# Reordering a hand-laid engine schedule in a gated-delta-rule and expert kernel

## The chip, the core and the metric

The kernel runs on one core of a Trainium2 chip. The metric is the device time of one execution in microseconds; lower is better. The core has five instruction queues that matter here: TensorE (PE, with its weight loads shown as PEld), VectorE (DVE), ScalarE (ACT), GpSimd (POOL) and SyncE (SP), which issues the DMAs. Each queue runs its instructions strictly in the order in which they were written; semaphores tie the queues together.

## What is computed

The reference is one transformer layer on 4 sequences of 256 tokens with 256 features: a gated delta rule attention with 16 key heads and 32 value heads of width 128, then a mixture of 34 small experts. Cut to what matters here:

```python
qkvz = x @ W_qkvz.T                      # 16 heads, 6*128 columns each
qkv  = silu(conv1d_causal(qkv, conv_w))  # 4 taps per channel
q, k = rmsnorm(q), rmsnorm(k)
M = strictly_lower(k_beta @ k.T * decay)
T = inverse(I + M)                       # solve_triangular in the reference
v_new = T @ v_beta - (T @ k_beta_exp_g) @ state
out   = q_exp_g @ state + (q @ k.T * decay) @ v_new
state = state * exp(g_last) + k_decayed.T @ v_new
y = (rmsnorm(out) * norm_w * silu(z)) @ W_out.T
x = x + layernorm(y)
x = x + layernorm(experts(layernorm(x)))
```

## The kernel before

The attention stage is cut into 64 **units**. A unit is one pair (group, batch): a group is one key head with its two value heads, and there are 16 groups of 4 batches, so a group has unit 0 to unit 3. The state is carried in two chunks of 128 tokens per unit.

Two streams of work run side by side in the attention stage.

The **unit stream** does the delta rule of one unit. Its backbone is a triangular inverse built up in seven levels, here called the ladder. For level n:

- TensorE forms `x n` (function `x`, L619) into `X_BANK`, from `n16` and the part `t16` of the inverse;
- ScalarE copies it to `x16`, called `xe n` (L954; the last one, `xe 6`, is L956);
- TensorE forms `w n` (L639 for one product, L647 for its transpose), from `x16` and `u16`;
- VectorE merges them with predicated copies, called `t n` (L1199) and `u n` (L1212, for `u 6` a plain copy, L1215).

`w 0` (L630, L632) opens the ladder of a unit. It overwrites the banks of the unit ahead and therefore waits for that unit's `u 6`. So ladders of two units never overlap. Between its rungs stand the other steps of the units just behind: the solve against the state (`y0` L663, `y1` L675 to L681, `y2` L687 on TensorE, `g` L966, `vn` L972 and `v0s` L979 on ScalarE, `rr` L1225 and `r1h` L1232 on VectorE), the carried product `p` (L696), the output `o` (L711, L714), the mean of squares (`sqr` L986 on ScalarE, `hsum` L1395 on GpSimd, `ss` L725 on TensorE, `ln` and `rex` L993 and L999 on ScalarE), the gating (`hz` L1241, `ht` L1250), the output projection `proj` (L734) and its accumulation `acc` (L1257). For the next unit there are the key products `kk` (L607, L610), `mask` (L1175), `cap`, `exp` and `cross` (L915, L929, L936 on ScalarE), the decayed matrix `nt` (L1184), its f16 copies `n16` (L943) and, on GpSimd, `nl` (L1413), the factors `at` (L1421) and `qx` (L1428), and `eye`, which resets `t16` and `u16` (L1403, L1407).

The **front stream** prepares the next group. It has 18 fills of two PSUM banks: `fill n` and `rest n` are the two halves of a projection of 512 tokens (L559, three products each), `evict n` is ScalarE's copy out of the bank (L858 or L864), and three `tap`s per fill on VectorE (L1139) are the convolution. Then come `silu` (L893, L898), squares on GpSimd, the norm (`nexp` L905, `nmul` L1167), transposes of v (`fill 14` to `fill 17`), the per-group scalars `sc` (L1160), and the split of the following group's weights into high and low f16 parts: `hi` on ScalarE (L886) and `lo` on VectorE (L1149). SiLU and the exponentials lie in different activation tables, and a group changes table four times (L893, L800, L864, L800).

What orders all this is not a scheduler but two tables of numbers. `SLOT` lists the steps of the unit stream once; an entry is a step, its index, and a lag in units (how many units behind the current one it belongs to). `FRONT` hangs the front stream's steps on places (unit within the group, position in `SLOT`), with the number of groups ahead. `sequence()` walks both and yields one global list. Each engine's program takes the steps that it owns out of that list, in order:

```python
def attention(engine_steps):
    for what, k, U in sequence():
        if what in engine_steps:
            engine_steps[what](U, k)
```

So a table entry matters only through the order that it gives among steps of the same engine. The waits stand inside the steps and are the same wherever a step stands.

Of the kernel before, what the change touches and what calls it, by code (L numbers as in the profile page):

```python
# [61 lines left out]

FRONT = {
    (0, 0): [("tap", 1, 1)],
    (0, 2): [("fill", 1, 1)],
# [2 lines left out]
    (0, 16): [("evict", 1, 1)],
    (0, 18): [("tap", 3, 1)],
    (0, 21): [("fill", 2, 1)],  # L70
    (0, 28): [("rest", 2, 1)],
    (0, 33): [("tap", 4, 1)],
    (0, 38): [("tap", 5, 1)],
# [5 lines left out]
    (0, 68): [("tap", 7, 1)],
    (0, 71): [("tap", 8, 1)],  # L80
    (0, 74): [("tap", 9, 1)],
    (1, 1): [("evict", 3, 1)],
    (1, 2): [("fill", 4, 1)],
    (1, 4): [("rest", 4, 1)],
    (1, 13): [("tap", 10, 1), ("evict", 4, 1)],
    (1, 16): [("fill", 5, 1)],
    (1, 18): [("tap", 11, 1)],
    (1, 27): [("evict", 5, 1)],
    (1, 28): [("rest", 5, 1)],
    (1, 30): [("tap", 12, 1)],  # L90
    (1, 38): [("tap", 13, 1)],
    (1, 46): [("tap", 14, 1)],
# [1 line left out]
    (1, 53): [("fill", 6, 1)],
    (1, 60): [("tap", 16, 1)],
    (1, 61): [("wo", 0, 1)],
    (1, 67): [("tap", 17, 1), ("rest", 6, 1), ("sq", 0, 1)],
    (1, 72): [("fill", 7, 1), ("tap", 18, 1)],
    (1, 74): [("evict", 6, 1)],
    (2, 4): [("tap", 19, 1)],  # L100
    (2, 5): [("rest", 7, 1)],
    (2, 10): [("fill", 8, 1), ("rest", 8, 1)],
    (2, 13): [("tap", 20, 1), ("evict", 7, 1)],
# [3 lines left out]
    (2, 21): [("tap", 23, 1), ("qsq", 0, 1), ("silu", 1, 1)],
    (2, 27): [("rest", 9, 1)],
    (2, 29): [("fill", 10, 1), ("silu", 2, 1)],
    (2, 31): [("rest", 10, 1), ("evict", 9, 1)],  # L110
    (2, 45): [("fill", 11, 1)],
# [1396 lines left out]
```

## Time and profile before

| | |
|---|---|
| median of 3 runs | 1440.54 us (1439.3 to 1442.4) |
| the profiled execution, its own time | 1435.98 us |
| its span, first to last instruction | 1433.7 us |
| PE busy | 1290.2 us (90%) |
| PE weight loads busy | 892.1 us (62%) |
| DVE busy | 1078.2 us (75%) |
| ACT busy | 961.3 us (67%) |
| POOL busy | 633.8 us (44%) |
| mean granted TensorE clock | 0.979 |

The attention stage fills the span up to about 1107 us and the experts run from there to the end. Busy shares over the span mix these two. Matmul ends are modelled and weight loads overlap matmuls, so the pitch between starts of neighbouring instructions, and idle time with its releaser, say more of TensorE than its busy share does.

### The profile page before, as it was taken

The numbers are of one execution on the slowest core, as the hardware profiler recorded it, in microseconds if no ns is written. First come the engines' busy times: TensorE is split into PE (matmuls) and PEld (weight loads), VectorE is DVE, ScalarE is ACT, GpSimd is POOL, SyncE is SP. The second block draws the span as 40 slices with busy tenths as digits, with TensorE's granted clock in tenths as the row PEclk, the third lists the DMA queues.
The fourth block names the chain that finished last, engine by engine and source line by source line (L and its number), as shares of the span: only waits on it lengthen the run. The fifth ranks groups of instructions, "written<-read, shape, count | busy, mean of one in ns | idle before, by whom it ended". The sixth has DMA issues, their size and how long they took to land.

```text
span 1433.7 us, 33842 instructions
## 1 busy us (share of the span) xinstructions
PE 1290.2 (90%) x11516; PEld 892.1 (62%) x11516; DVE 1078.2 (75%) x2142; ACT 961.3 (67%) x2122; POOL 633.8 (44%) x726
## 2 busy tenths in 40 slices
...
DMA packets 44656, 76.34 MB, mean 53 GB/s; under 512 B 7172, under 2 KB 26022, under 8 KB 44488
## 3 DMA queue, kind: packets, MB, share of 16 engines
...
q14 instruction: 73, 0.60, 0.1%
...
## 4 chain that ended last, share of the span: by engine, by line
PE 65%; DVE 17%; issue 8%; ACT 8%; DVEq 1%; DMA 0%; SPq 0%; POOL 0%; ACTq 0%; POOLq 0%
PE bank L559 11%; PE bank L781 8%; PE products L734 6%; DVE sil L1139 6%; PE bank L514 5%; PE products L514 4%; PE products L711 4%; PE bank L639 4%; PE products L725 3%; PE products L607 3%; PE bank L619 3%; PE bank L647 3%; DVE u L1212 2%; DVE t L1199 2%; PE bank L696 2%
## 5 line engine op out<-in xcount | busy, mean ns | idle before, releaser
L559 PE MATMUL bank<-xT,whl 128*128 128x512 f16 x1152 | 305.9, 380 | 12.8 <-DVE sil L1139 12.7
L1139 DVE SCALAR_TENSOR_TENSOR sil<-bank,cw,sil 128x510 f32<-128x510 f32 (+2 forms) x384 | 283.7, 739 | 9.9 <-ACT sil L858 5.3
L1403 POOL COPY t<-eye 128x512 f16<-128x512 f16 x64 | 39.2, 612 | 446.9 <-PE bank L647 446.9
L1199 DVE CAST_PREDICATED t<-levm,bank 128x256 f16<-128x256 uint8 x384 | 166.0, 432 | 87.2 <-PE bank L632 52.9
L954 ACT ACTIVATE x<-bank 128x256 f16<-128x256 f32 x320 | 125.5, 392 | 93.2 <-PE bank L619 89.5
L1029 ACT ACTIVATE kq<-vtok 128x512 f16<-128x512 f32 x94 | 59.2, 630 | 192.0 <-DVE vtok L1326 192.0
L1212 DVE CAST_PREDICATED u<-levm,bank 128x256 f16<-128x256 uint8 x384 | 163.6, 426 | 0.3
L619 PEld LDWEIGHTS bank<-t,n 128*128 128x128 f16 x1536 | 78.0, 97 | 103.7 <-DVE t L1199 78.3
L559 PEld LDWEIGHTS bank<-xT,whl 128*128 128x128 f16 x1152 | 92.4, 98 | 78.0 <-DVE sil L1139 16.7
L781 PE MATMUL bank<-wmhl,kq 128*128 128x256 f16 x1128 | 138.3, 273 | 0.3 <-DVE kq L1332 0.2
L619 PE MATMUL bank<-t,n 128*128 128x64 f16 x1536 | 110.0, 194 | 25.4 <-DVE t L1199 23.9
L781 PEld LDWEIGHTS bank<-wmhl,kq 128*128 128x128 f16 x1128 | 110.2, 98 | 33.2 <-DVE kq L1332 1.1
L734 PE MATMUL products<-wo,hT 128*128 128x256 f32 x512 | 128.0, 393 | 2.2 <-DVE hT L1250 2.2
L639 PEld LDWEIGHTS bank<-x,u 128*128 128x128 f16 x1280 | 62.6, 97 | 96.1 <-ACT x L954 87.4
L647 PE MATMUL bank<-u,x 128*128 128x64 f16 (+1 forms) x1536 | 109.9, 194 | 6.0 <-ACT x L956 5.1
L639 PE MATMUL bank<-x,u 128*128 128x64 f16 x1280 | 90.9, 193 | 24.3 <-ACT x L954 9.4
L734 PEld LDWEIGHTS products<-wo,hT 128*128 128x128 f32 x512 | 93.4, 193 | 13.2 <-DVE hT L1250 2.9
L858 ACT ACTIVATE sil<-bank,cw 128x512 f32<-128x512 f32 x128 | 88.5, 692 | 17.5 <-PE bank L559 15.8
L1395 POOL TENSOR_TENSOR hsq<-hsq,qsq 128x512 f32<-128x512 f32 x64 | 81.4, 1272 | 39.2 <-ACT hsq L986 39.1
L1421 POOL TENSOR_TENSOR at<-kqm,ex 128x256 f32<-128x256 f32 x128 | 93.8, 733 | 7.8 <-ACT ex L929 7.8
L1440 POOL TENSOR_SCALAR wms<-wms 128x512 f32<-128x512 f32 x47 | 31.7, 675 | 143.4 <-DMA wms<-wm 143.4
L1428 POOL TENSOR_TENSOR qx<-cross,exb 128x256 f32<-128x256 f32 x128 | 93.6, 731 | 2.9 <-ACT exb L923 2.9
...
## 6 DMA issues: line engine op xcount, KB each, us to landing
...
```

Of the source, the lines that this page charges most:

```text
L514: mm = nc.tensor.matmul(dst, stationary(h, k), moving(l, k), start=(n == 0), stop=(n == len(terms) - 1))
L559: mm = nc.tensor.matmul(dst[:, :], whl[:, h, k, col:col + HD], xT[:, l, k, half * 512:(half + 1) * 512], start=(k == 0 and m == 0), stop=( ...
L619: mm = nc.tensor.matmul(X_BANK[:, m * 64:(m + 1) * 64], N[:, m], r, start=True, stop=True)
L639: mm = nc.tensor.matmul(X_BANK[:, m * 64:(m + 1) * 64], Ut[:, m], halves(X, n)[:, m, :, 0], start=True, stop=True)
L647: mm = nc.tensor.matmul(o, l, r, start=True, stop=True)
L734: mm = nc.tensor.matmul(KB_BANK[:, c * D:(c + 1) * D], hT[:, pair(U), v, c], wo[:, q, v], start=(v == 0), stop=(v == 1))
L781: mm = nc.tensor.matmul(bank[4 + t // 2][:, (t % 2) * D:(t % 2 + 1) * D], hid[:, n % HR, h, m * P:(m + 1) * P], wmhl[:, k % HLR, l, D:2 * ...
L954: ins = nc.scalar.mul(halves(X, n)[:, :, :, 0], packed(X_BANK, n), -1.0)
L1139: nc.vector.scalar_tensor_tensor(out=dst[:, :, late:S], in0=src[:, :, 0:S - late], scalar=cw[:, q, i, 3 - late:4 - late], in1=dst[:, :, la ...
L1199: nc.vector.copy_predicated(halves(t16[:, pair(U)], n)[:, :, :, 0], by4(2 * n, n), packed(X_BANK, n)).then_inc(s_tup, 1)
L1212: nc.vector.copy_predicated(halves(Ut, n)[:, :, :, 1], by4(2 * n + 1, n), packed(WT_BANK, n)).then_inc(s_uup, 1)
L1421: nc.gpsimd.tensor_tensor(at[:, third(U), v], kqm[:, w, :, 1], ex[:, w, v], ALU.mult).then_inc(s_at, 1)
```

## The change

Only the two tables change: the order of `SLOT` and the places in `FRONT`, with some lags that stay equivalent for the data flow. No step is added or removed, no wait is changed, no buffer is resized. The table is three lines longer, so every later line number is higher by 3 in the changed kernel (L1199 becomes L1202). A few entries of the diff, to show their form and the steps spoken of below:

```diff
--- before.py
+++ after.py
@@ -49,90 +49,93 @@
...
-SLOT = [("n16", 0, 0), ("sqr", 0, 2), ("g", 0, 1), ("x", 1, 0), ("u", 0, 0), ("nl", 0, 0), ("xe", 1, 0), ("w", 1, 0),
-        ("ss", 0, 2), ("x", 2, 0), ("y1", 0, 1), ("exb", 0, 0), ("w", 2, 0), ("eye", 1, -1), ("t", 1, 0), ("u", 1, 0),
-        ("xe", 2, 0), ("ln", 0, 2), ("rex", 0, 2), ("xe", 3, 0), ("v0s", 0, 1), ("rr", 0, 1), ("t", 2, 0),
-        ("x", 3, 0), ("hz", 0, 2), ("u", 2, 0), ("y2", 0, 1), ("ht", 0, 2), ("t", 3, 0), ("w", 3, 0), ("eye", 0, -2),
-        ("at", 1, 0), ("p", 0, 1), ("x", 4, 0), ("u", 3, 0), ("qx", 1, 0), ("hsum", 0, 1), ("proj", 0, 2),
-        ("at", 0, -1), ("vn", 0, 1), ("r1h", 0, 1), ("cap", 0, -1), ("xe", 4, 0), ("row", 0, 4), ("y0", 1, 1),
-        ("w", 4, 0), ("acc", 0, 2), ("t", 4, 0), ("kk", 0, -1), ("u", 4, 0), ("x", 5, 0), ("g", 1, 1),
-        ("mask", 0, -1), ("cap", 1, -1), ("rr", 1, 1), ("qx", 0, -1), ("t", 5, 0), ("xe", 5, 0), ("y1", 1, 1),
-        ("w", 5, 0), ("exp", 0, -1), ("cross", 0, -1), ("xe", 6, 0), ("u", 5, 0), ("nt", 0, -1), ("x", 6, 0),
-        ("y2", 1, 1), ("w", 6, 0), ("o", 0, 1), ("w", 0, -1), ("u", 6, 0), ("vn", 1, 1), ("y0", 0, 0), ("t", 0, -1)]
+SLOT = [("vn", 1, 2), ("w", 6, 1), ("n16", 0, 0), ("at", 0, 0), ("sqr", 0, 2), ("o", 0, 2), ("w", 0, 0),
+        ("exb", 0, 0), ("xe", 1, 0), ("y0", 0, 1), ("t", 1, 0), ("g", 0, 1), ("u", 1, 0), ("x", 1, 0), ("w", 1, 0),
+        ("ss", 0, 2), ("x", 2, 0), ("xe", 2, 0), ("rr", 0, 1), ("ln", 0, 2), ("y1", 0, 1), ("t", 2, 0), ("hz", 0, 2),
+        ("at", 1, 0), ("row", 0, 1), ("w", 2, 0), ("rex", 0, 2), ("hsum", 0, 1), ("eye", 1, -2), ("xe", 3, 0),
+        ("u", 2, 0), ("y2", 0, 1), ("ht", 0, 2), ("v0s", 0, 1), ("x", 3, 0), ("t", 3, 0), ("w", 3, 0), ("vn", 0, 1),
+        ("u", 3, 0), ("p", 0, 1), ("x", 4, 0), ("proj", 0, 2), ("qx", 0, 0), ("xe", 4, 0), ("r1h", 0, 1),
+        ("y0", 1, 1), ("w", 4, 0), ("acc", 0, 2), ("t", 4, 0), ("u", 4, 0), ("kk", 0, -1), ("x", 5, 0), ("y1", 1, 1),
+        ("w", 5, 0), ("mask", 0, -1), ("rr", 1, 1), ("qx", 1, 0), ("t", 5, 0), ("u", 5, 0), ("cap", 0, -1),
+        ("cap", 1, -1), ("g", 1, 1), ("nl", 0, -1), ("nt", 0, -1), ("y2", 1, 1), ("xe", 5, 0), ("eye", 0, -3),
+        ("u", 6, 0), ("x", 6, 0), ("exp", 0, -1), ("t", 0, -1), ("cross", 0, -1), ("xe", 6, 0), ("u", 0, -1)]
 
 FRONT = {
...
-    (0, 2): [("fill", 1, 1)],
+    (0, 2): [("evict", 0, 1)],
...
-    (0, 14): [("tap", 2, 1)],
...
-    (0, 39): [("evict", 2, 1)],
-    (0, 41): [("weights", 1, -1)],
...
-    (1, 51): [("tap", 15, 1), ("silu", 0, 1)],
...
-    (2, 15): [("tap", 21, 1), ("owts", 0, 0)],
...
-    (2, 46): [("silu", 3, 1), ("cw", 0, 2)],
...
-    (3, 6): [("sc", 0, 1)],
...
-    (3, 45): [("lo", 1, 1), ("evict", 16, 1)],
...
-    (3, 64): [("fill", 0, 2)],
...
+    (0, 14): [("evict", 1, 1)],
+    (0, 25): [("owts", 0, 0)],
...
+    (0, 40): [("cw", 0, 2)],
...
+    (0, 54): [("evict", 2, 1)],
...
+    (1, 41): [("silu", 0, 1)],
...
+    (1, 61): [("weights", 1, 0)],
...
+    (2, 29): [("sc", 0, 1)],
...
+    (3, 52): [("lo", 1, 1)],
+    (3, 53): [("fill", 0, 2)],
...
+    (3, 71): [("fill", 1, 2)],
...
```

What this does to the queues is read from the instruction lists. Three places matter. In them `sil<-bank,cw,sil` is a tap, `t<-levm,bank` and `u<-levm,bank` are `t n` and `u n`, `bank<-xT,whl` on TensorE is half of a projection fill, `x<-bank` on ScalarE is `xe n`, `ex<-grow,sc` is a `cap` pair, and `y<-bank` is `g`.

VectorE, unit 0 of a steady group, from the unit's `u 6` of the unit ahead to level 1. Before:

```order
L1215 CAST u<-bank 64x4x64
L1139 SCALAR_TENSOR_TENSOR sil<-bank,cw,sil 128x2x255
L1199 COPY_PREDICATED t<-levm,bank 128x256
L1139 SCALAR_TENSOR_TENSOR sil<-bank,cw,sil 128x2x254
L1212 COPY_PREDICATED u<-levm,bank 128x256
L1139 SCALAR_TENSOR_TENSOR sil<-bank,cw,sil 128x2x253
L1199 COPY_PREDICATED t<-levm,bank 128x128x2
L1212 COPY_PREDICATED u<-levm,bank 128x128x2
```

Changed:

```order
L1218 CAST u<-bank 64x4x64
L1142 SCALAR_TENSOR_TENSOR sil<-bank,cw,sil 128x2x255
L1142 SCALAR_TENSOR_TENSOR sil<-bank,cw,sil 128x2x254
L1202 COPY_PREDICATED t<-levm,bank 128x256
L1215 COPY_PREDICATED u<-levm,bank 128x256
L1142 SCALAR_TENSOR_TENSOR sil<-bank,cw,sil 128x2x253
L1202 COPY_PREDICATED t<-levm,bank 128x128x2
L1215 COPY_PREDICATED u<-levm,bank 128x128x2
```

The first tap pair now stands ahead of `t 0`, and `u 0` follows `t 0` directly. Unit 1 has the same move around its `t 0`; unit 2 keeps a tap between the two, and in unit 2 the copy `sc<-scal` now stands between `hz` and `u 2`, where before it stood in unit 3 between `u 0` and `t 1`. In unit 3 the second `whl<-wt,whl` (`lo 1`) has moved from ahead of `acc` to behind `u 4`.

TensorE, from the key products of a unit 0 to the output product of the unit before the last. Before:

```order
L681 MATMUL bank<-y,eye 128x256
L639 MATMUL bank<-x,u 128x64 x4
L647 MATMUL bank<-u,x 128x64 x4
L559 MATMUL bank<-xT,whl 128x512 x3
L619 MATMUL bank<-t,n 128x64 x4
L687 MATMUL bank<-rr,u 128x128 x2
L559 MATMUL bank<-xT,whl 128x512 x3
L647 MATMUL bank<-u,x 64x64 x4
L711 MATMUL products<-at,vn 128x128 x2
L714 MATMUL products<-qx,v0s 128x128
```

Changed:

```order
L684 MATMUL bank<-y,eye 128x256
L562 MATMUL bank<-xT,whl 128x512 x3
L642 MATMUL bank<-x,u 128x64 x4
L650 MATMUL bank<-u,x 128x64 x4
L562 MATMUL bank<-xT,whl 128x512 x3
L690 MATMUL bank<-rr,u 128x128 x2
L622 MATMUL bank<-t,n 128x64 x4
L562 MATMUL bank<-xT,whl 128x512 x3
L650 MATMUL bank<-u,x 64x64 x4
L714 MATMUL products<-at,vn 128x128 x2
```

Three projection halves now stand in this stretch where before there were two: one between `y1` and `w 5`, one between `w 5` and `y2`, and one between `x 6` and `w 6`. `y2` has gone ahead of `x 6`. In the changed order the half that came behind `w 0` (`fill 1`) is thus issued ahead of it. Likewise `y2` of the first chunk stands ahead of `x 3` in every unit.

ScalarE, unit 1 of a steady group, from `xe 3` to `xe 6`. Before:

```order
L972 COPY vn<-bank 128x2x128
L915 ACTIVATE ex<-grow,sc 128x128 x2
L954 ACTIVATE x<-bank 128x16x16
L893 ACT_TABLE_LOAD
L893 ACTIVATE sil<-sil 128x1024
L966 CAST y<-bank 128x256
L915 ACTIVATE ex<-grow,sc 128x128 x2
L954 ACTIVATE x<-bank 128x8x32
L800 ACT_TABLE_LOAD
L929 ACTIVATE ex<-ex 128x512
L936 COPY cross<-products 128x256
L956 ACTIVATE x<-bank 128x4x64
```

Changed:

```order
L975 COPY vn<-bank 128x2x128
L896 ACT_TABLE_LOAD
L896 ACTIVATE sil<-sil 128x1024
L957 ACTIVATE x<-bank 128x16x16
L861 ACTIVATE sil<-bank,cw 128x512
L918 ACTIVATE ex<-grow,sc 128x128 x4
L969 CAST y<-bank 128x256
L957 ACTIVATE x<-bank 128x8x32
L803 ACT_TABLE_LOAD
L932 ACTIVATE ex<-ex 128x512
L939 COPY cross<-products 128x256
L959 ACTIVATE x<-bank 128x4x64
```

The table load with the first SiLU has gone ahead of `xe 4`, the projection's eviction behind it, and both `cap` pairs ahead of the guess copy `y<-bank`, which now stands directly ahead of `xe 5`. The set of instructions between `xe 3` and `xe 6` is the same.

On GpSimd both `at` halves now come ahead of `hsum` and both `qx` halves behind it. On SyncE the load of the next weights stands behind one more row load, and the load of `wo` comes a unit earlier.

## Rows read from the trace of the kernel before

**Rows 1.** Page, part 4: chain that ended last, shares of the span by engine

```profile
PE 65%; DVE 17%; issue 8%; ACT 8%; DVEq 1%; DMA 0%; SPq 0%; POOL 0%; ACTq 0%; POOLq 0%
```

**Rows 2.** Windows: stretch, length, then busy us (instructions) per engine, clock, DMA share, GB/s

```profile
456.00:521.00 65.00, 62.48 (x596) 43.65 (x596) 55.22 (x112) 54.83 (x125) 31.45 (x36) 1.00 0.11 33
```

**Rows 3.** One line's instructions, VectorE L1175: ns min/median/max, first and last start

```profile
L1175 DVE TENSOR_TENSOR kqm<-products,cst x64: 677/692/694, 65.6 to 1091.3; 128x512 f32<-128x512 f32 x64
```

**Rows 4.** Timeline, TensorE: the first product (w0) of five units in a row

```profile
525.58 0.28 PE L630 MATMUL bank<-eye,n 128*128 128x64 f16 x4
...
540.72 0.28 PE L630 MATMUL bank<-eye,n 128*128 128x64 f16 x4
...
556.45 0.28 PE L630 MATMUL bank<-eye,n 128*128 128x64 f16 x4
...
575.48 0.28 PE L630 MATMUL bank<-eye,n 128*128 128x64 f16 x4
...
591.24 0.28 PE L630 MATMUL bank<-eye,n 128*128 128x64 f16 x4
```

**Rows 5.** Timeline, all engines, 525 to 528 us: start, us, engine, line

```profile
525.77 0.60 ACT L986 ACTIVATE hsq<-products 128x512 f32<-128x512 f32 x1 [0.58 <-PE products L714]
...
526.51 1.28 POOL L1395 TENSOR_TENSOR hsq<-hsq,qsq 128x512 f32<-128x512 f32 x1 [0.15 <-ACT hsq L986]
...
526.98 0.38 ACT L954 ACTIVATE x<-bank 128x256 f16<-128x256 f32 x1 [0.34 <-PE bank L619]
...
527.14 0.44 DVE L1212 CAST_PREDICATED u<-levm,bank 128x256 f16<-128x256 uint8 x1
...
527.73 0.28 PE L639 MATMUL bank<-x,u 128*128 128x64 f16 x4
...
527.97 1.10 PE L725 MATMUL products<-hsq,cst 128*128 128x256 f32 x4
```

**Rows 6.** Timeline, 532 to 568 us: out product L734 and accumulation L1257, two units

```profile
532.72 1.97 PE L734 MATMUL products<-wo,hT 128*128 128x256 f32 x8
...
535.07 0.68 DVE L1257 TENSOR_TENSOR acc<-acc,products 128x512 f32<-128x512 f32 x1
...
565.79 1.97 PE L734 MATMUL products<-wo,hT 128*128 128x256 f32 x8
...
567.80 0.69 DVE L1257 TENSOR_TENSOR acc<-acc,products 128x512 f32<-128x512 f32 x1 [1.50 <-PE products L734]
```

**Rows 7.** Timeline, ScalarE, 546 to 556 us

```profile
546.12 0.38 ACT L954 ACTIVATE x<-bank 128x256 f16<-128x256 f32 x1
...
548.74 1.28 ACT L893 ACT_TABLE_LOAD   x1
...
551.25 0.69 ACT L915 ACTIVATE ex<-grow,sc 128x128 f32<-128x128 f32 x2
...
554.31 0.39 ACT L956 ACTIVATE x<-bank 128x256 f16<-128x256 f32 x1
```

**Rows 8.** Timeline, TensorE, 520 to 525 us; in brackets idle before and releaser

```profile
521.96 0.29 PE L639 MATMUL bank<-x,u 128*128 128x64 f16 x4 [0.26 <-ACT x L954]
...
522.21 0.81 PE L559 MATMUL bank<-xT,whl 128*128 128x512 f16 x3
```

**Rows 9.** Chain that ended last, in order of time: start, us, piece

```profile
522.37 0.65 PE bank L559 x3
```

**Rows 10.** One line's instructions each, L1149, L1413, L1160: ns min/median/max

```profile
L1149 DVE SCALAR_TENSOR_TENSOR whl<-wt,whl x32: 951/954/1357, 15.3 to 979.4; 128x768 f16<-128x768 f32 x32
...
L1413 POOL TENSOR_TENSOR nl<-nt,n x64: 1148/1161/1889, 71.0 to 1098.8; 128x512 f16<-128x512 f32 x64
...
L1160 DVE COPY sc<-scal x16: 185/1078/1081, 51.5 to 1037.4; 128x64 f32<-128x64 f32 x16
```

**Rows 11.** Timeline, VectorE and GpSimd, 577 to 582 us

```profile
578.62 0.73 POOL L1428 TENSOR_TENSOR qx<-cross,exb 128x256 f32<-128x256 f32 x1
...
578.81 1.35 DVE L1149 SCALAR_TENSOR_TENSOR whl<-wt,whl 128x768 f16<-128x768 f32 x1
```

More of the change, by code:

```diff
@@ L63 @@
 FRONT = {
-    (0, 0): [("tap", 1, 1)],
-    (0, 2): [("fill", 1, 1)],
+    (0, 2): [("evict", 0, 1)],
     (0, 7): [("rest", 1, 1)],
-    (0, 14): [("tap", 2, 1)],
[L68 to L73, printed above, removed]
-    (0, 39): [("evict", 2, 1)],
-    (0, 41): [("weights", 1, -1)],
-    (0, 45): [("tap", 6, 1)],
-    (0, 61): [("fill", 3, 1)],
-    (0, 67): [("rest", 3, 1)],
@@ L79 @@
[L79 to L92, printed above, removed]
-    (1, 51): [("tap", 15, 1), ("silu", 0, 1)],
@@ L94 @@
[L94 to L103, printed above, removed]
-    (2, 15): [("tap", 21, 1), ("owts", 0, 0)],
-    (2, 16): [("tap", 22, 1), ("fill", 9, 1)],
-    (2, 19): [("evict", 8, 1)],
@@ L107 @@
[L107 to L111, printed above, removed]
-    (2, 46): [("silu", 3, 1), ("cw", 0, 2)],
-    (2, 48): [("rest", 11, 1)],
-    (2, 53): [("evict", 10, 1), ("evict", 11, 1)],
-    (2, 64): [("fill", 14, 1)],
-    (2, 67): [("fill", 12, 1)],
-    (2, 71): [("fill", 13, 1)],
-    (2, 72): [("evict", 14, 1)],
-    (3, 1): [("evict", 12, 1)],
@@ L120 @@
-    (3, 2): [("hi", 0, 1)],
-    (3, 5): [("fill", 15, 1)],
-    (3, 6): [("sc", 0, 1)],
-    (3, 7): [("evict", 13, 1)],
-    (3, 16): [("fill", 16, 1), ("evict", 15, 1)],
-    (3, 18): [("lo", 0, 1)],
-    (3, 24): [("nexp", 0, 1)],
-    (3, 29): [("fill", 17, 1)],
-    (3, 36): [("hi", 1, 1)],
-    (3, 41): [("nmul", 0, 1)],
-    (3, 45): [("lo", 1, 1), ("evict", 16, 1)],
-    (3, 56): [("evict", 17, 1)],
-    (3, 64): [("fill", 0, 2)],
-    (3, 67): [("rest", 0, 2)],
-    (3, 71): [("tap", 0, 2)],
@@ L135 @@
-    (3, 74): [("evict", 0, 2)],
+    (0, 9): [("tap", 2, 1)],
+    (0, 13): [("tap", 3, 1)],
+    (0, 14): [("evict", 1, 1)],
+    (0, 25): [("owts", 0, 0)],
+    (0, 27): [("fill", 2, 1)],
+    (0, 35): [("rest", 2, 1)],
+    (0, 40): [("cw", 0, 2)],
+    (0, 42): [("tap", 4, 1)],
+    (0, 47): [("tap", 5, 1)],
+    (0, 50): [("tap", 6, 1)],
+    (0, 54): [("evict", 2, 1)],
+    (0, 55): [("fill", 3, 1)],
+    (0, 59): [("tap", 7, 1)],
+    (0, 66): [("tap", 8, 1)],
+    (0, 70): [("tap", 9, 1)],
@@ new lines @@
+    (0, 73): [("rest", 3, 1)],
+    (1, 2): [("evict", 3, 1)],
+    (1, 9): [("evict", 4, 1), ("tap", 10, 1)],
+    (1, 10): [("fill", 4, 1)],
+    (1, 14): [("rest", 4, 1), ("tap", 11, 1)],
+    (1, 35): [("fill", 5, 1)],
+    (1, 38): [("tap", 12, 1), ("rest", 5, 1)],
+    (1, 41): [("silu", 0, 1)],
+    (1, 43): [("tap", 13, 1)],
+    (1, 47): [("tap", 14, 1)],
+    (1, 50): [("tap", 15, 1)],
+    (1, 55): [("fill", 6, 1), ("evict", 5, 1)],
+    (1, 58): [("wo", 0, 1)],
+    (1, 60): [("sq", 0, 1)],
@@ new lines @@
+    (1, 61): [("weights", 1, 0)],
+    (1, 63): [("tap", 16, 1), ("qsq", 0, 1)],
+    (1, 67): [("tap", 17, 1)],
+    (1, 70): [("tap", 18, 1)],
+    (1, 73): [("tap", 19, 1)],
+    (1, 74): [("rest", 6, 1)],
+    (2, 2): [("evict", 6, 1)],
+    (2, 9): [("tap", 20, 1), ("fill", 7, 1)],
+    (2, 12): [("tap", 21, 1)],
+    (2, 14): [("evict", 7, 1), ("rest", 7, 1), ("tap", 22, 1)],
+    (2, 17): [("fill", 8, 1), ("tap", 23, 1)],
+    (2, 19): [("rest", 8, 1)],
+    (2, 27): [("evict", 8, 1), ("fill", 9, 1)],
```

27 lines of the change are left out of this document (added).

## The prediction

> **What bounds the kernel now.** I read the chain of waits first: TensorE holds 65% of the chain that ended last, VectorE 17%, ScalarE 8% [rows 1]. Then the windows: in 65 us of the steady attention stage TensorE shows 62.5 us busy at full clock, VectorE 55.2, ScalarE 54.8, GpSimd 31.5 [rows 2]. So TensorE is close to full, but not by throughput alone, since three other engines stand in its loop. The `mask` product is issued 64 times between 65.6 and 1091.3 us [rows 3], 16.3 us a unit, so the part that the change touches is some 1026 of the 1434 us; the experts behind it keep their order. The timeline gives the shape of a group: five `w 0` in a row start 15.14, 15.73, 19.03 and 15.76 us apart, 65.66 us a group [rows 4]. The heaviest unit 2 takes most projection halves and most SiLU work.
>
> TensorE waits for other engines at small places, not at one large one. An example is `w 5`, which stands idle 0.26 us for `xe 5` while a projection half that could have run is queued behind it [rows 8]. A half takes 0.65 us of the chain [rows 9]. In units 1 and 2 ScalarE is full: between `xe 3` at 546.12 and `xe 6` at 554.31 us it runs the same set of instructions in both kernels, with a table load of 1.28 us among them [rows 7], and no idle time is printed at the rows of that stretch. There an order of ScalarE's own cannot shorten anything; it can only open a hole.
>
> **The change, part by part.** Nothing is added or removed. All costs are differences of waiting, and I count them from `w 0` to `w 0`, unit by unit.
>
> *Unit 0.* The first hand-off of the ladder: `u 0` starts at 527.14, ends at 527.58, and `w 1` follows at 527.73, so an end becomes a TensorE start in 0.15 us [rows 5]. A tap stands ahead of that `u 0` now and not in the changed order. Then `xe 1` decides, which ends at 527.36: `w 1` could start at 527.51, 0.22 us earlier. But `ss` is next but for `w 1` itself, and it needs the sum on GpSimd, which starts at 526.51 and takes 1.28 us, to 527.79. It starts at 527.97 [rows 5]; with the same hand-off it could start at 527.94 at the earliest, and with a somewhat shorter one at 527.87. Behind it stands `x 2`. So of 0.22 us I count 0.05. Next, `acc` starts 2.01 us after `proj` where VectorE is idle, and 2.35 us after it in unit 0, where a third tap stands ahead of it [rows 6]. That tap goes behind `u 4`. `kk` needs `acc`; I count 0.15 of the 0.34 us, as `kk` has work of its own to start with. Against these, a tap more stands ahead of `u 6` at the end of the unit, for which `w 0` waits. `w 0` also stands behind the output products, which cover most of it; when that cover is gone the tap costs at least the 0.34 us that one makes at `acc` [rows 6], and I count 0.10. Sum: 0.10 us gained.
>
> *Unit 1.* The same hand-off gains at `w 1`, and `ss` here is freed 0.1 us earlier relative to `w 0`, because the later `u 6` delays `w 0` but not the chain by GpSimd. Then ScalarE's full stretch begins, and TensorE's place in it is set by `xe 3`. `rest 5` has moved behind `w 3` and so delays `p`, `x 4` and `proj` by about what was gained; that is hidden by the SiLU that now stands ahead of `xe 4`. I count 0.05 us gained.
>
> *Unit 2.* ScalarE is full again, the tap stays between `t 0` and `u 0`, and `y2` ahead of `x 3` adds its two products. I count 0.05 us lost.
>
> *Unit 3.* TensorE does one projection half more here (0.65 us, [rows 9]) and one less in unit 0. It has bubbles to take it: 0.26 us printed at `w 5` [rows 8], as much again behind `x 6`, where the next product waits for `xe 6`. The half ahead of `w 5` is longer than its bubble and delays `w 5`, by 0.4 us at most. Since all of the half that finds no bubble would otherwise have been run in unit 0, where TensorE waits at `w 1`, the balance is small. The later `lo 1` can put `mask` back by up to its 0.95 us [rows 10], but `nt` behind it also waits for ScalarE's exponential, which hides it; I put the uncovered part at nothing, and at 0.4 us as the upper bound. I count 0.15 us gained.
>
> *The low part `lo 0`.* It normally takes 0.95 us and at most 1.36 [rows 10]. In unit 3 it took 1.35, having started while a `qx` was on GpSimd, and `nl` right behind took up to 1.89 where 1.16 is usual [rows 10, 11]. VectorE and GpSimd hold each other up. `lo 0` stands directly ahead of `rr`, `t 2` and so of TensorE's `x 3`. With GpSimd's new order it starts later within a `qx`, and the long `nl` is no longer behind it. Its gain lies between 0 and 0.40 us, less than nothing if it hits a full `qx`; I take 0.15, near the middle, since only its start within the other instruction is unknown. The Trainium skill, SBUF — State Buffer, section "Who interferes with whom", states that a VectorE instruction with two SBUF inputs and a GpSimd instruction that reads SBUF exclude each other for the whole instruction. By that rule the pair can only be waited out, so by it the term is 0.40 if GpSimd is idle and 0 if a `qx` has just begun.
>
> *GpSimd and SyncE.* Both `qx` halves (0.73 us each, [rows 11]) now come behind `hsum`, which ends at 527.79 [rows 5], so they are done by about 530. `p` stands shortly ahead of `proj`, which starts at 532.72 [rows 6]. That slack of some 2 us hides them; without it they would hold `p` directly. The weights' load is issued when `lo 1` is done in both orders, and the row load now ahead of it waits for steps of a unit 3, which are done by then. The start and the tail of the stage keep their order nearly: nothing.
>
> **Sum.** 0.10 + 0.05 − 0.05 + 0.15 + 0.15 = 0.40 us a group, times 15 groups that have a front stream beside them: 6.0 us. The profiled execution took 1435.98 us (span 1433.7), which would become 1430.0. It lies 4.6 us below the median of the runs; the median 1440.54 becomes 1434.5 us. About 0.2% (2.9 us) is what a measurement of this kernel can tell from no change.
>
> **The rivals.**
>
> *Slower: a hole in ScalarE's full stretch.* In units 1 and 2 a `cap` pair stood between `g` and `xe 5` and filled the time until `x 5` was done; one pair takes 0.69 us [rows 7]. Now both come ahead of `g`. If they end before `x 5`, ScalarE idles up to that 0.69 us and everything to `xe 6` and the next `w 0` shifts with it; if they end after it, `y1` waits for `g` and holds up `w 5` behind it on TensorE. It decides from the point where either is off by more than 0.2 us. At 0.45 us, two thirds of a pair, in each of two units: 0.9 − 0.4 = 0.5 us a group, 7.5 us, 1448. For it: no idle time is left there now. Against it: the sum of ScalarE's work is unchanged.
>
> *Same: the gains are absorbed.* `ss` stays with the chain by GpSimd, ScalarE's stretches stay as long, and only 0.10 us a group is left: 1.5 us, 1439. For it: every gain above is smaller than a hand-off of 0.15 us or rests on two.
>
> *Faster by more: TensorE's bubbles close.* If the moved halves all land in idle time, the 0.65 us that unit 0 no longer holds is gained in full beside the sum: about 1.0 us a group, 15 us, 1425.5. For it: 0.26 us idle is printed at one place alone. Against it: the ladder's own latency, not TensorE's work, sets units 0 and 3.
>
> *Slower, from the shared port.* `sc` takes 0.19 us at best and 1.08 at the median [rows 10]: most of the time it waits out a GpSimd instruction. Before, it stood where VectorE had time. Now it stands ahead of `u 2` in unit 2. If GpSimd is at work then (scaling `wo`), `u 2` and `w 3` are up to 0.9 us late, of which I take 0.5 as uncovered: 7.5 us lost against 6 gained, 1442. The rule of the skill's SBUF page above is the general form of this; by it, a single GpSimd instruction at that moment is enough.
>
> **How the numbers follow.** The forecast (0.2 to 0.7 us a group) has 0.45; absorbed 0.20; faster by more 0.12; the hole in ScalarE 0.17; the port 0.06. That makes 0.55 for faster by over 0.2%, 0.22 within it, 0.23 for slower (the port case lies on the border). The range runs from 1424, where the bubbles close, to 1446, where the hole costs 0.35 a unit and nothing is gained with it. The forecast's own range is 1430 to 1437.5.
>
> **What would show it.** Right: the distance of `mask` products falls to about 65.2 us a group, by most from unit 3; `w 1` comes 0.2 us earlier after `w 0` in unit 0 but `ss` does not; `lo 0` shorter than 1.35 us; `sc` at 0.2 us; ScalarE without idle time from `xe 3` to `xe 6` in unit 1, and that stretch still 8.2 us. Wrong: idle time of ScalarE ahead of `xe 5` (the hole), TensorE waiting at L678 for `g`, `sc` at 1.08 us, `p` waiting for `qx`, or unit 2 longer than 19.2 us.

## The result, and the profile after

| | before | changed |
|---|---|---|
| median of 20 runs each, same chips | 1440.99 us (1436.05 to 1443.21) | 1438.3 us (1435.13 to 1440.68) |
| span of the profiled execution | 1433.7 us | 1432.9 us |
| first `w 0`, last `w 0` | 68.15, 1095.23 us | 67.97, 1092.64 us |
| DVE busy | 1078.2 us | 1063.5 us |

The ratio is 0.9981, with a 95% interval of 0.9972 to 0.9990: 2.7 us shorter, 0.19%. That is a real gain, and less than half of the 6.0 us forecast. The time lies inside the range, beside the 1439 of the rival in which the gains are absorbed; but that rival had 0.10 us a group, and 0.26 was measured.

The chain by engine, from the page of the changed kernel, answers to [rows 1]:

```profile
PE 66%; DVE 16%; ACT 8%; issue 8%; DVEq 1%; DMA 0%; SPq 0%; ACTq 0%; POOL 0%; POOLq 0%
```

The same 65 us window as [rows 2]. TensorE is as full as it was, and VectorE has lost 1.1 us of waiting inside its instructions:

```profile
456.00:521.00 65.00, 62.49 (x604) 45.06 (x602) 54.09 (x112) 55.31 (x125) 31.55 (x36) 1.00 0.11 35
```

The timeline of TensorE, five `w 0` in a row, answers to [rows 4]. They stand 15.12, 15.70, 19.11 and 15.50 us apart, 65.43 together, where it was 65.66:

```profile
525.25 0.28 PE L633 MATMUL bank<-eye,n 128*128 128x64 f16 x4
...
540.37 0.28 PE L633 MATMUL bank<-eye,n 128*128 128x64 f16 x4
...
556.07 0.28 PE L633 MATMUL bank<-eye,n 128*128 128x64 f16 x4
...
575.18 0.28 PE L633 MATMUL bank<-eye,n 128*128 128x64 f16 x4
...
590.68 0.28 PE L633 MATMUL bank<-eye,n 128*128 128x64 f16 x4
```

All 64 `w 0` can be read in this way. In the steady groups a unit repeats within some 0.03 us, except for a few in a run: in every kernel unit 1 of one or two groups is 0.35 us longer, some units are off by 0.1 or 0.15, and unit 3 of group 14 is about 14.8. So a table of unit lengths, the medians over groups 1 to 14 of one profiled execution, tells kernels apart far more finely than their times do. "First group" is from the first `w 0` to the fifth.

| kernel | unit 0 | unit 1 | unit 2 | unit 3 | sum | first group |
|---|---|---|---|---|---|---|
| before | 15.14 | 15.73 | 19.04 | 15.77 | 65.68 | 63.41 |
| changed | 15.02 | 15.79 | 19.11 | 15.50 | 65.42 | 64.53 |

A steady group is 0.26 us shorter, and the first one is 1.12 us longer. The last `w 0` comes 2.59 us earlier, near the 2.7 us of the medians. That they are so near is in part luck: a second profile of the changed kernel (`changed_again` below) has its last `w 0` at 1094.38 us, 0.85 us earlier than before, and most of the difference lies in the first group. What follows the last `w 0` (338.5 us before, 340.3 after) differs from run to run: over all profiles of this study, with the experts' order the same in each, it lies between 338.5 and 342.4 us. So I judge the rest by `w 0`, not by spans.

**What went as said.** In unit 0 `w 1` starts 1.85 us after `w 0` (2.15 before, [rows 5]). `acc` follows `proj` by 2.01 us, without the third tap ahead of it (2.35 before, [rows 6]). ScalarE's row shows `w 1` now waits for `xe 1`:

```profile
526.66 0.38 ACT L957 ACTIVATE x<-bank 128x256 f16<-128x256 f32 x1 [0.30 <-PE bank L622]
...
527.10 0.29 PE L642 MATMUL bank<-x,u 128*128 128x64 f16 x4 [0.47 <-ACT x L957]
```

In unit 3 `lo 0` takes 0.97 us where it took 1.35 [rows 11]. It starts in the last part of a `qx`, not in the first:

```profile
577.97 2.14 POOL L1431 TENSOR_TENSOR qx<-cross,exb 128x256 f32<-128x256 f32 x2
...
578.55 0.97 DVE L1152 SCALAR_TENSOR_TENSOR whl<-wt,whl 128x768 f16<-128x768 f32 x1
```

**What did not.** The timeline of ScalarE in unit 1 answers to [rows 7]. From `xe 3` (545.47) to `xe 6` (553.93) it takes 8.46 us where it took 8.19, and `xe 5` waits 0.18 us for `x 5`. Counted from `w 0`, `xe 3` comes 0.19 us earlier than before, which is the gain of the hand-offs; the stretch behind it then loses 0.27. The table load and the SiLU (546.65 to 549.0) now stand ahead of `xe 4` (548.90), and both `cap` pairs (549.74) and `g` (550.91) ahead of `xe 5`:

```profile
545.47 0.38 ACT L957 ACTIVATE x<-bank 128x256 f16<-128x256 f32 x1
...
546.65 1.28 ACT L896 ACT_TABLE_LOAD   x1
547.94 1.06 ACT L896 ACTIVATE sil<-sil 128x1024 f32<-128x1024 f32 x1
548.90 0.37 ACT L957 ACTIVATE x<-bank 128x256 f16<-128x256 f32 x1
...
549.74 1.27 ACT L918 ACTIVATE ex<-grow,sc 128x128 f32<-128x128 f32 x4
550.91 0.36 ACT L969 CAST y<-bank 128x256 f16<-128x256 f32 x1
551.45 0.38 ACT L957 ACTIVATE x<-bank 128x256 f16<-128x256 f32 x1 [0.18 <-PE bank L622]
...
553.93 0.39 ACT L959 ACTIVATE x<-bank 128x256 f16<-128x256 f32 x1
```

And the first unit of the first group is 14.61 us long where it was 13.11. Four windows of the changed kernel at its beginning (stretch, length, busy time per engine, and third from the end TensorE's granted clock) show TensorE busy 0.74 of 2 us, and then for 4 us near the lower of its two levels, 1.2 GHz (0.5 of full speed). The kernel before has 1.00 in all of them, in the one profile that was taken of it.

```profile
70.00:72.00 2.00, 0.74 (x13) 0.51 (x14) 1.67 (x4) 1.13 (x3) 0.00 (x0) 1.00 0.23 77
72.00:74.00 2.00, 2.00 (x17) 1.00 (x18) 0.88 (x3) 0.28 (x1) 0.00 (x0) 0.61 0.03 8
74.00:76.00 2.00, 1.55 (x15) 0.84 (x13) 0.65 (x2) 0.10 (x1) 0.00 (x0) 0.54 0.00 0
76.00:78.00 2.00, 1.52 (x17) 1.28 (x14) 1.89 (x5) 1.84 (x6) 0.00 (x0) 1.00 0.00 0
```

### The profile page after: what moved, and what is told of

It reads as the page before. It is cut to its first block, busy times and chain, and to the rows that moved or that the text cites. A ratio compares the mean times of both kernels' runs of the same rounds, so it can differ in the third digit from the quotient of the medians.

```text
span 1432.9 us, 33842 instructions
## 1 busy us (share of the span) xinstructions
PE 1291.2 (90%) x11516; PEld 912.4 (64%) x11516; DVE 1063.5 (74%) x2142; ACT 964.8 (67%) x2122; POOL 633.9 (44%) x726
## 4 chain that ended last, share of the span: by engine, by line
PE 66%; DVE 16%; ACT 8%; issue 8%; DVEq 1%; DMA 0%; SPq 0%; ACTq 0%; POOL 0%; POOLq 0%
PE bank L562 13%; PE bank L784 8%; PE products L737 7%; DVE sil L1142 5%; PE bank L517 5%; PE products L517 4%; PE products L714 4%; PE products L728 3%; PE products L610 3%; PE bank L642 3%; PE bank L622 3%; PE bank L650 3%; DVE u L1215 2%; PE bank L699 2%; PE products L717 2%
## 5 line engine op out<-in xcount | busy, mean ns | idle before, releaser
L1202 DVE CAST_PREDICATED t<-levm,bank 128x256 f16<-128x256 uint8 x384 | 166.3, 433 | 103.8 <-PE bank L642 64.8
L622 PEld LDWEIGHTS bank<-t,n 128*128 128x128 f16 x1536 | 81.1, 98 | 55.6 <-DVE t L1202 26.7
L1431 POOL TENSOR_TENSOR qx<-cross,exb 128x256 f32<-128x256 f32 x128 | 100.9, 811 | 0.0
L650 PEld LDWEIGHTS bank<-u,x 128*128 128x128 f16 (+1 forms) x1536 | 72.4, 100 | 40.3 <-ACT x L959 40.3
```

Source lines behind the costliest of these rows:

```text
L622: mm = nc.tensor.matmul(X_BANK[:, m * 64:(m + 1) * 64], N[:, m], r, start=True, stop=True)
L650: mm = nc.tensor.matmul(o, l, r, start=True, stop=True)
L1202: nc.vector.copy_predicated(halves(t16[:, pair(U)], n)[:, :, :, 0], by4(2 * n, n), packed(X_BANK, n)).then_inc(s_tup, 1)
L1431: nc.gpsimd.tensor_tensor(qx[:, third(U), v], cross[:, w], exb[:, w, v].unsqueeze(1).to_broadcast([P, 2, P]), ALU.mult).then_inc(s_qx, 1)
```

## Experiments

**One engine at a time.** Each engine walks the sequence by itself, so an engine can keep the old order while another takes the new one. These kernels hold both tables, and each engine's call says which it walks:

```diff
-def sequence():
+def sequence(SLOT, FRONT):
...
-        def attention(engine_steps):
-            for what, k, U in sequence():
+        def attention(engine_steps, new=True):
+            for what, k, U in sequence(*((SLOT, FRONT) if new else (SLOT_OLD, FRONT_OLD))):
...
-                       "o": o, "ss": ss, "proj": proj})
+                       "o": o, "ss": ss, "proj": proj}, new=False)
```

TensorE alone:

> TensorE alone walks the changed table; the other four engines keep the order before. Counted from `w 0` to `w 0` in the steady groups (before: 15.14, 15.73, 19.03, 15.76 = 65.67; changed kernel: 65.44). Theory A (the moved projection halves are what shortens unit 3, and `rest 5` behind `w 3` and `rest 11` ahead of `w 4` are what lengthens units 1 and 2): unit 3 falls by 0.1 or more, units 1 and 2 rise by 0.05 to 0.1 each. Theory B (TensorE's order is nearly free, since it waits for others anyway): every unit within 0.05 of before. Rival C (TensorE's order only fits the order of the others): the group becomes longer than before by over 0.3.

VectorE alone:

> VectorE alone walks the changed table. Theory A (the tap behind `u 0` and the third tap behind `u 4` gain on VectorE alone): unit 0 shorter by about 0.1, and `lo 0` still 1.35 us because GpSimd's `qx` is where it was. Theory B (the gain of `lo 0` comes from VectorE reaching it later or earlier, not from GpSimd's order): `lo 0` at about 0.97 us here and unit 3 shorter by 0.25. Rival C: the taps that stand late in unit 0 find no gap in an old TensorE order, unit 0 is longer by 0.3 or more.

ScalarE alone:

> ScalarE alone walks the changed table. Theory A: in units 1 and 2 it is full, so its order can only open a hole there: both units the same or longer by up to 0.1, idle time ahead of `xe 5`. Units 0 and 3 within 0.05. At the start of the stage, where `evict 0` of the next group now stands early, the first group stays at 63.4 us. Rival: the hole is ScalarE's alone and larger without TensorE's changed order (`x 4`, `x 5` come when they came before, while both `cap` pairs are done): 0.2 us or more in each of the two units.

GpSimd and SyncE alone:

> GpSimd and SyncE alone walk the changed table (both `qx` behind `hsum`). Theory A (shared port, decided by where GpSimd's `qx` stands): `lo 0` at 0.97 instead of 1.35 us and `nl` never over 1.2 us, unit 3 shorter by 0.25, the other units within 0.05, so a group of 65.4: all of the change's steady gain. Theory B (what VectorE does ahead of `lo 0` decides): `lo 0` stays at 1.35, the group at 65.65. Rival C: `qx` that late delays `p`, units longer by 0.1 or more.

| changed order on | unit 0 | unit 1 | unit 2 | unit 3 | sum | first group |
|---|---|---|---|---|---|---|
| none (before) | 15.14 | 15.73 | 19.04 | 15.77 | 65.68 | 63.41 |
| TensorE | 15.07 | 16.71 | 19.21 | 15.92 | 66.91 | 65.45 |
| VectorE | 15.04 | 15.67 | 19.03 | 15.78 | 65.52 | 63.77 |
| ScalarE | 15.16 | 15.82 | 19.03 | 15.76 | 65.77 | 63.75 |
| GpSimd, SyncE | 15.15 | 15.73 | 19.03 | 15.46 | 65.37 | 63.11 |
| all (changed) | 15.02 | 15.79 | 19.11 | 15.50 | 65.42 | 64.53 |

GpSimd's order gives 0.31 us, all of it in unit 3, and there `lo 0` takes 0.99: theory A. Its gain alone is larger than that of the whole change. VectorE's order gives 0.10 in unit 0 and 0.06 in unit 1, with `lo 0` at 1.35 as before: theory A. ScalarE's order costs 0.09 in unit 1 and nothing in unit 2, so theory A held in its size; its stretch from `xe 3` to `xe 6` is 8.28 us. No idle time is printed ahead of its `xe 5`, but the views print none under 0.15 us, and these rows point to a short wait:

```profile
552.81 0.36 ACT L1056 CAST y<-bank 128x256 f16<-128x256 f32 x1
...
552.85 0.28 PE L709 MATMUL bank<-t,n 128*128 128x64 f16 x4
...
553.16 0.38 ACT L1044 ACTIVATE x<-bank 128x256 f16<-128x256 f32 x1
```

`xe 5` starts 0.31 us after `x 5`, as closely as where it is printed as waiting (0.32 in the changed kernel), and 0.35 us after `y<-bank`, where it is 0.26 from a `y<-bank` to the row behind it in the kernel before. Its first group is 63.75 us, 0.35 longer than expected.

TensorE's order alone costs 1.23 us a group, rival C. Unit 3 is 0.15 us longer, not shorter, so the moved halves by themselves do not shorten it. Most of the cost, 0.98 us, is in unit 1. There ScalarE in its old order wants `evict 5` ahead of `vn` and `xe 4`, while TensorE now delivers that piece behind `w 3`. ScalarE's timeline of that run:

```profile
488.80 0.62 ACT L1069 ACTIVATE v0s<-bank,sc 128x128 f32<-128x128 f32 x2
490.28 0.69 ACT L948 ACTIVATE sil<-bank,cw 128x512 f32<-128x512 f32 x1 [0.87 <-PE bank L649]
```

So TensorE's and ScalarE's new orders need each other, and the other two don't need them. That points to a version that leaves both out.

**The gains without the costs, and the first group.** The first kernel keeps TensorE and ScalarE on the old table (`new=False` for both). The second does that too, and the third is the changed kernel; both start by the old table and go over to the new one behind the four units of the first group:

```diff
+    done = set()
+    for step in walk(SLOT_OLD, FRONT_OLD, 4):
+        done.add(step)
+        yield step
+    for step in walk(SLOT, FRONT):
+        if step not in done:
+            yield step
```

> GpSimd, SyncE and VectorE walk the changed table, TensorE and ScalarE the order before. Theory A (the two gains are separate: GpSimd's 0.30 us in unit 3, VectorE's 0.10 and 0.07 us in units 0 and 1; TensorE's and ScalarE's new orders only cost): 15.04, 15.66, 19.03, 15.46 = 65.20 us a group, 0.24 less than with the whole change. Theory B (they overlap, or VectorE's order needs TensorE's to pay): 65.4 or more. The first group is 0.1 to 0.4 us longer than with the old order.

> As the kernel before in this list, but VectorE, GpSimd and SyncE keep the old order until the units of the first group have begun, and go over to the changed one there. Theory A (VectorE's order at the entry of the stage, its two taps ahead of `t 0`, is what costs there): the first `w 0` at 68.2 us and the first group at 63.1 us. Theory B (the first group's time is set by the clock that happens to be granted in a run): it can come out at 63.8 or more here too.

> The changed kernel, with all five engines in the old order until the first group's units have begun. Steady groups unchanged at 65.44. Theory A (the 1.12 us lost in the first group come from the order there): the first group falls from 64.53 to 63.1 to 63.4 us and TensorE's granted clock stays 1.00 between 68 and 80 us. Theory B (a clock dip of that one run): the group stays at 64 or more, or the dip comes at another place.

The fourth moves two projection halves back in the changed kernel's table:

```diff
-    (1, 38): [("tap", 12, 1), ("rest", 5, 1)],
+    (1, 36): [("rest", 5, 1)],
+    (1, 38): [("tap", 12, 1)],
...
-    (2, 43): [("fill", 11, 1), ("rest", 11, 1)],
+    (2, 43): [("fill", 11, 1)],
...
-    (2, 47): [("evict", 10, 1)],
+    (2, 47): [("rest", 11, 1), ("evict", 10, 1)],
```

> The changed kernel with two projection halves of TensorE put back: `rest 5` ahead of `w 3` in unit 1, `rest 11` behind `w 4` in unit 2. Theory A (these two moves make the hole of ScalarE in units 1 and 2): unit 1 falls from 15.80 by 0.10 to 0.25, no idle time ahead of `xe 5` in it, unit 2 falls from 19.12 to 19.03. Theory B (the order of `cap` and `g` on ScalarE makes it): both units stay within 0.03.

| kernel | unit 0 | unit 1 | unit 2 | unit 3 | sum | first group (its unit 0, 1) |
|---|---|---|---|---|---|---|
| pool_dve | 15.04 | 15.66 | 19.04 | 15.47 | 65.21 | 64.92 (13.51, 16.91) |
| pool_dve_start | 15.04 | 15.65 | 19.03 | 15.46 | 65.18 | 64.81 (13.10, 16.91) |
| all_start | 15.03 | 15.79 | 19.11 | 15.50 | 65.43 | 64.83 (13.11, 16.93) |
| rests | 15.03 | 15.92 | 19.03 | 15.50 | 65.48 | 64.68 (14.59, 15.56) |

The gains of GpSimd and VectorE add up to the hundredth: 65.21 where 65.20 was expected, theory A. In `rests`, unit 2 falls by 0.08 to 19.03, as expected: `rest 11` ahead of `w 4` is what unit 2 lost (both halves were moved in one kernel; that each acts in its own unit is argued, not shown). Unit 1 rises by 0.13 instead of falling: my cause for it was wrong. ScalarE still waits ahead of `xe 5`, longer than in the changed kernel:

```profile
487.09 0.38 ACT L958 ACTIVATE x<-bank 128x256 f16<-128x256 f32 x1 [0.30 <-PE bank L623]
```

With `rest 5` ahead of `w 3`, VectorE reaches `u 3` 0.4 us later, and with it both taps, `acc`, `t 4` and `u 4`. In this kernel the half is better behind `w 3`. The first group keeps its dip, at 72 to 78 us.

In `pool_dve_start` the first `w 0` is at 68.22 us and unit 0 of the first group takes 13.10 us, against 13.51 in `pool_dve`: theory A holds for that unit, and VectorE's order at the entry costs 0.4 us there. The group as a whole (64.81) is as theory B allowed. In `all_start` unit 0 is 13.11 us again, and TensorE's clock is 1.00 there. But in both kernels a dip comes 18 us later, and takes 1.4 us in unit 1 (`all_start`):

```profile
72.00:74.00 2.00, 1.52 (x21) 0.76 (x19) 1.54 (x4) 0.46 (x2) 1.31 (x2) 1.00 0.56 129
74.00:76.00 2.00, 1.06 (x15) 0.50 (x13) 1.17 (x3) 1.73 (x5) 0.00 (x0) 1.00 0.04 8
90.00:92.00 2.00, 1.51 (x13) 1.33 (x14) 2.00 (x6) 1.99 (x3) 0.00 (x0) 0.74 0.00 0
92.00:94.00 2.00, 2.00 (x9) 1.26 (x9) 0.68 (x2) 0.93 (x4) 0.00 (x0) 0.50 0.02 4
```

The group is as long as before the start was put back, so each theory has half of it: the dip at 72 us is gone with the order, and its absence does not keep another away. `pool_dve_start` runs the first group's units 0 and 1 with the steps that `pool_only` runs on TensorE, ScalarE and VectorE; one has the dip at 90 us and one has none.

**The best version timed, the port, and two further tests.**

> The same kernel as pool_dve (GpSimd, SyncE and VectorE on the changed table, TensorE and ScalarE on the one before), now timed in rounds. Counted from its steady groups it is 15 x 0.47 = 7.0 us shorter than the kernel before, less about 1 us in the first group: 6 us, a ratio of 0.9958, where the changed kernel measured 0.9981. If the gain of the steady groups is eaten elsewhere (the clock at the start or in the experts), it lies at 0.998 as well. The dip of the clock at 90 us of its first profile comes again if it belongs to the order, and is gone or elsewhere if it is chance.

> The kernel before with one swap on GpSimd alone: `nl` behind the copy of `eye 1` that followed it, so `nl` starts 0.6 us later; `qx` and `at` stay. Theory A (it is `nl`, not `qx`, that `lo 0` meets: in the kernel before `nl` took 1.88 us beside it, in pool_only `lo 0` lay wholly beside two `qx` and took 0.99): `lo 0` falls to 0.95 to 1.0 us, the longest `nl` to 1.2, unit 3 from 15.76 to 15.46, all of pool_only's gain. Theory B (my prediction's: `lo 0` is held up by the `qx` that runs when it starts): `lo 0` stays at 1.35 and unit 3 at 15.76.

```diff
-SLOT = [("n16", 0, 0), ("sqr", 0, 2), ("g", 0, 1), ("x", 1, 0), ("u", 0, 0), ("nl", 0, 0), ("xe", 1, 0), ("w", 1, 0),
-        ("ss", 0, 2), ("x", 2, 0), ("y1", 0, 1), ("exb", 0, 0), ("w", 2, 0), ("eye", 1, -1), ("t", 1, 0), ("u", 1, 0),
+SLOT = [("n16", 0, 0), ("sqr", 0, 2), ("g", 0, 1), ("x", 1, 0), ("u", 0, 0), ("eye", 1, -1), ("xe", 1, 0), ("w", 1, 0),
+        ("ss", 0, 2), ("x", 2, 0), ("y1", 0, 1), ("exb", 0, 0), ("w", 2, 0), ("nl", 0, 0), ("t", 1, 0), ("u", 1, 0),
```

> The changed kernel itself, once more. If the dip of TensorE's clock at 72 to 76 us belongs to TensorE's changed order at the entry (it is there in three of three kernels that have that order), it comes again and the first group takes 64.5 us; if it is chance, the first group takes 63.1 to 63.6 or the dip lies elsewhere. The steady groups again 65.44.

> The changed kernel with TensorE alone put back to the old order. Theory A (ScalarE's order, the SiLU with its table load ahead of `xe 4`, is what costs unit 1; TensorE's order costs units 2 and 3 a little): 15.04, 15.75 to 15.82, 19.03, 15.46, a group of 65.3. Theory B (TensorE's order is what costs unit 1 as well): 15.66 there and the group at 65.2. Rival C: ScalarE and TensorE fit each other only together, and unit 1 is 16 or more, as when TensorE changed alone (16.71, ScalarE idle 0.87 us ahead of `evict 5`).

| kernel | unit 0 | unit 1 | unit 2 | unit 3 | sum | first group (its unit 0, 1) |
|---|---|---|---|---|---|---|
| pool_dve_5 | 15.04 | 15.66 | 19.03 | 15.47 | 65.20 | 63.47 (13.51, 15.46) |
| nl_behind_eye | 15.14 | 15.75 | 19.04 | 15.78 | 65.71 | 64.87 (13.10, 16.96) |
| changed_again | 15.02 | 15.79 | 19.11 | 15.50 | 65.42 | 65.87 (15.95, 15.30) |
| pe_old | 15.04 | 15.71 | 19.03 | 15.49 | 65.27 | 64.71 (13.42, 16.78) |

The first is the kernel of `pool_dve` again; in the second GpSimd's `nl` and `eye 1` change places; the third is the changed kernel itself; in the fourth TensorE's call has `new=False`.

`pool_dve_5` took 1433.15 us (median of 9) against 1440.0 of the kernel before (median of 14), a ratio of 0.9958 with an interval of 0.9945 to 0.9970. That is the expected number, and beats the changed kernel's 0.9981: the intervals don't overlap. The dip at 90 us of its first profile is gone, and one at 63 to 71 us, ahead of the first `w 0`, has taken its place.

`nl_behind_eye` falls for theory B, my prediction's. `lo 0` still takes 1.35 us, and the delay passes from `nl` to the short copy that now follows `qx`. GpSimd and VectorE of that run, in unit 3:

```profile
516.79 0.73 POOL L1428 TENSOR_TENSOR qx<-cross,exb 128x256 f32<-128x256 f32 x1
517.46 1.34 POOL L1407 COPY u<-eye 128x512 f16<-128x512 f16 x1
...
516.98 1.35 DVE L1149 SCALAR_TENSOR_TENSOR whl<-wt,whl 128x768 f16<-128x768 f32 x1
```

The copy takes 0.61 us elsewhere, so 0.73 more. Each waits for the other to end: `lo 0`, issued at 516.98, gets on when `qx` ends at 517.52, and the copy gets on when `lo 0` has ended. What `lo 0` loses is the part of `qx` that is left when it starts, less some 0.14 us: here 0.54 us is left and 0.40 lost. In the changed order some 0.13 us is left and 0.02 lost, and the second `qx` takes the wait instead (the pair 2.14 us, where it takes 1.42 in unit 0), and nobody needs it soon. The Trainium skill, SBUF — State Buffer, section "Who interferes with whom", has this rule, that the two engines exclude each other for the whole instruction; by that rule, the trace agrees, in both directions, but for those 0.14 us.

`changed_again` has the dip again, between 72 and 82 us, and longer:

```profile
72.00:74.00 2.00, 1.52 (x18) 0.76 (x17) 1.44 (x4) 0.49 (x2) 0.00 (x0) 0.89 0.03 8
74.00:76.00 2.00, 1.56 (x11) 0.78 (x9) 0.48 (x2) 0.27 (x1) 0.00 (x0) 0.50 0.00 0
76.00:78.00 2.00, 1.52 (x14) 1.27 (x15) 1.89 (x4) 1.56 (x5) 0.00 (x0) 0.50 0.00 0
78.00:80.00 2.00, 2.00 (x7) 1.37 (x5) 1.10 (x3) 0.56 (x2) 0.00 (x0) 0.50 0.00 0
```

So all four profiles with TensorE's new order at the entry of the stage (the changed kernel twice, `pe_only`, `rests`) have a dip that begins at 72 to 74 us, and none of the ten with the old one does. That one belongs to the order. The timeline of TensorE in the changed kernel shows what stands ahead of it. `fill 1` has gone ahead of `w 0`, so of the two halves that stood among the first products only one is left, and TensorE waits four times in a row, where it waited twice:

```profile
69.46 0.29 PE L622 MATMUL bank<-t,n 128*128 128x64 f16 x4 [0.43 <-DVE t L1202]
70.22 0.30 PE L642 MATMUL bank<-x,u 128*128 128x64 f16 x4 [0.48 <-ACT x L957]
...
71.20 0.29 PE L622 MATMUL bank<-t,n 128*128 128x64 f16 x4 [0.56 <-DVE t L1202]
71.97 0.30 PE L642 MATMUL bank<-x,u 128*128 128x64 f16 x4 [0.47 <-ACT x L957]
...
72.22 1.25 PE L562 MATMUL bank<-xT,whl 128*128 128x512 f16 x3
...
82.58 0.28 PE L633 MATMUL bank<-eye,n 128*128 128x64 f16 x4 [1.47 <-DVE u L1218]
```

The row at 72.22 is a projection half of 0.81 us at full clock. In the steady groups `ss` and the `y` products of the units ahead fill some of these places; in the first group there are no such units. That these waits bring the dip is argued, not shown: the kernel before has TensorE busy for 0.86 us from 70 to 72 and for 0.67 us from 74 to 76 us, and no dip.

The loss of that first unit can be split by comparing starts, counted from `w 0`, with the kernel before. At `w 2` the changed kernel is 0.12 us behind, at `x 4`, after the dip, 1.30, and at `w 6` 0.85. The last 0.65 us are the wait of the next `w 0` for `u 6` (the last row above), behind VectorE's taps. Before, that wait was shorter:

```profile
81.26 0.28 PE L630 MATMUL bank<-eye,n 128*128 128x64 f16 x4 [0.82 <-DVE u L1215]
```

`dve_only` has the same 1.47 us there, without a dip in its first group, and a first unit of 13.50 us. So the dip is the larger part, VectorE's taps most of the rest, and the four waits cost little by themselves.

**Does the changed kernel lose time at the start?** The one profile of the kernel before is a lucky yardstick, for it has no dip in its first 100 us. Seven of the ten profiles with TensorE's old order at the entry have one or two, at 60 to 72 or at 90 to 96 us, and none of the four with the new order has one at those places. The first group takes 64.5 to 65.9 us with the new order; with the old one it takes 63.1 to 63.8 in five profiles, and 64.7 to 64.9 in the five with a dip at 90 us. Counted from the start of the span, the fifth `w 0` comes at 132.5 to 134.4 us with the new order and at 131.3 to 135.3 with the old one. So that the new order has its dip at 72 us is shown; that the changed kernel loses 1.1 us at its start in a typical execution is not.

`pe_old` lies between its theories: 15.71 in unit 1. Against the 15.66 of `pool_dve`, ScalarE's order costs 0.05 there, and TensorE's 0.08 more in the changed kernel. Units 2 and 3 give back 0.08 and 0.01 when TensorE's order is undone.

## Why the prediction was wrong

**The direction held, the sum did not.** Against 0.40 us a group, 0.26 was measured. Of the missing 0.14 us, 0.11 is unit 1, the step that failed most clearly. Two terms of unit 3, one wrong and one too small, cancel. The other part is the start: it was put at nothing, and 1.12 us was lost there between the two first profiles. Fourteen groups at 0.25 us, less that, and with the first `w 0` 0.18 us earlier, are the 2.6 us by which the last one is earlier. How much the start costs in a typical execution stays open: 14 groups at 0.25 us alone make 3.5 us, which lies inside the interval of the measured gain (1.4 to 4.0 us) as well as 2.7 does.

- *Unit 0, 0.10 gained:* right. Measured 0.12, of which VectorE's order alone gives 0.10. Its three terms (0.05, 0.15 and −0.10) were not measured apart. `w 1` comes 0.30 us earlier where 0.22 was forecast, and `ss` behind it, as forecast, much less (0.12).
- *Unit 1, 0.05 gained:* the step that failed by sign, 0.06 lost. VectorE's part is there (0.06 gained, by itself), but I took `rest 5` and the SiLU ahead of `xe 4` for a pair that hides itself, and ScalarE's stretch to stay at 8.2 us; it took 8.46. In the changed kernel ScalarE's order costs 0.05 and TensorE's 0.08, with 0.18 us of idle time ahead of `xe 5`. That is the rival of a hole at less than half of its 0.45 us. In unit 2 the wait ahead of `xe 5` was 0.16 us before already and is 0.24 now. Which move of TensorE's makes the 0.08 of unit 1 is open: it is not `rest 5`, for putting that back made the unit longer.
- *Unit 2, 0.05 lost:* 0.07 lost, by `rest 11`, which the prediction did not count. `y2` ahead of `x 3`, which it did count, still stands there in `rests`, and unit 2 is as before.
- *Unit 3, 0.15 for the projection half:* wrong. GpSimd's order alone gives 0.31, the whole change 0.27, and TensorE's order is worth nothing (15.50 with it, 15.49 in `pe_old` without it) or, by itself, 0.15 lost. "It has bubbles to take it" is true, but a bubble that is filled does not shorten the ladder that makes it.
- *`lo 0`, 0.15:* right in its mechanism and mis-sized; 0.38 us shorter, and 0.31 of that reached the unit. That the two errors of unit 3 cancel (0.30 forecast, 0.27 measured) is luck.
- *"The start and the tail of the stage keep their order nearly: nothing":* the units of the last group agree to 0.01 us, the start does not. There I compared the lists and not what the taps and halves wait for when no unit is ahead. Against the kernel before, which had no dip, the first group was 1.12 us longer in one profile and, with a longer dip, 2.46 us in the other; how much of this is the order's in a typical execution is open, as said above.
- *`sc` in unit 2:* 0.26 us at the median of its 16 instructions where it was 1.08, and at most 0.61. The port rival did not come about.
- *The upper end of the range, 1446:* it does not follow from its own terms. A hole of 0.35 us in each of two units, with nothing gained, is 0.7 us a group or 10.5 us, and gives 1451; 1446 is one hole of 0.35 a group.
